# Edges of a graph kernel laid out on 128 partitions by 1568 columns instead of 125 by 1600

## What is computed

```
src[200000], dst[200000]: node numbers;  edge_weight1[200000, 1]: edge length
deg   = segment_sum(1, dst) + 1
agg   = segment_sum(h[src] * norm[:, None], dst)            # twice; message layer alike
alpha = softmax over the edges of a dst; out = segment_sum(h[src] * alpha, dst)
logit = q[src] . k[dst] + silu(len * We1 + be1) @ We2 + be2  # softmax over the edges of a src
out   = segment_sum(v[dst] * softmax(logit) * cut(len), src)
```

## Time and profile before

| what | value |
|---|---|
| median of three runs | 23871.3 us |
| span of the profiled execution | 20599.5 us |
| POOL busy | 13905.9 us, 68% of the span |
| first scatter phase, POOL's first to last DMA | 566.1 to 3111.1 us |
| second scatter phase, POOL's first to last DMA | 3119.1 to 5549.0 us |

### The profile page before, as it was taken

How to read it: one execution, slowest core, us unless ns; L and a number is a source line. 1 busy time by engine, 2 the same in 40 slices (tenths; PEclk the granted TensorE clock), 3 DMA queues, 4 the chain that set the end, 5 groups by cost and what they waited for, 6 DMA issues and landing times. The chain is left out here.

```text
span 20599.5 us, 263453 instructions
## 1 busy us (share of the span) xinstructions
PE 11568.2 (56%) x38052; PEld 7949.2 (39%) x38053; DVE 9032.9 (44%) x32383; ACT 3681.9 (18%) x13726; POOL 13905.9 (68%) x14023
## 2 busy tenths in 40 slices
PE   4452005666644443444377778998477757734444
PEld 1221003333333333333222227888444446633333
DVE  7894000000133333333477776555455556643332
ACT  0000001111100000000088882222111111100000
POOL 0787777777667774777477777777377764437774
PEclk8655555555555555555599995555555556655555
DMA  0000000000112222222210002222355553312222
GB/s 19 1 2 2 2 2 10 2 2 2 13 49 53 53 53 40 53 52 53 30 8 2 2 2 48 54 54 54 76 157 156 157 126 100 100 34 53 53 53 39
DMA packets 955238, 936.26 MB, mean 45 GB/s; under 512 B 316676, under 2 KB 792417, under 8 KB 954328
## 3 DMA queue, kind: packets, MB, share of 16 engines
q0 software_dynamic: 448512, 670.29, 16.4%
q1 hardware_dynamic: 506112, 260.47, 4.7%
q10 hardware_dynamic: 576, 5.11, 0.1%
HBM read 788.96 MB, written 142.48 MB: 45 GB/s over the span
## 5 line engine op out<-in xcount | busy, mean ns | idle before, releaser
L941 PE MATMUL banks<-room 128*128 128x128 f32 (+2 forms) x16640 | 4717.8, 440 | 3647.6 <-DMA room<-tab,stage 3229.5
L847 POOL DMA_INDIRECT room<-tab,stage x4992 | 4710.4, 944 | 2189.1 <-issue 1513.5
L941 PEld LDWEIGHTS banks<-room 128*128 128x128 f32 x16640 | 3802.2, 316 | 4499.0 <-DVE room L954 2419.1
L964 DVE TENSOR_TENSOR acc<-acc,banks 128x128 f32 (+2 forms) x4160 | 1209.2, 291 | 5088.1 <-PE banks L941 4484.8
L954 DVE TENSOR_SCALAR room<-ramp,loc 128x128 f32<-128x128 f32 x11648 | 3173.8, 331 | 80.5 <-issue 66.0
L419 POOL DMA_INDIRECT by_src<-room,stage x1600 | 2058.9, 1287 | 1051.4 <-ACT room L410 567.5
L419 POOL DMA_INDIRECT by_dst<-room,stage x1600 | 1905.0, 1191 | 532.9 <-issue 487.0
L847 POOL DMA_INDIRECT acc<-tab_kv,stage x1664 | 1580.2, 950 | 785.1 <-issue 498.6
L847 POOL DMA_INDIRECT room<-tab_a,stage x1664 | 1571.6, 944 | 755.8 <-issue 405.0
L847 POOL DMA_INDIRECT room<-tab_h,stage x1664 | 1575.1, 947 | 535.5 <-issue 500.8
L939 PE MATMUL banks<-acc,room 128*128 128x512 f32 x3328 | 1627.4, 611 | 497.7 <-ACT acc L887 451.3
(11 more groups left out here) (263 smaller groups left out, 11748.5 us busy)
## 6 DMA issues: line engine op xcount, KB each, us to landing
value_rows<-acc SPq DMA_DIRECT2D x416, 256.0 KB, 3.0
room<-value_rows SPq DMA_DIRECT2D x416, 256.0 KB, 2.9
room<-tab,stage POOLq DMA_INDIRECT x4992
room<-tab_a,stage POOLq DMA_INDIRECT x1664
room<-tab_h,stage POOLq DMA_INDIRECT x1664
acc<-tab_kv,stage POOLq DMA_INDIRECT x1664
by_src<-room,stage POOLq DMA_INDIRECT x1600, 2.6
by_dst<-room,stage POOLq DMA_INDIRECT x1600, 2.6
```

The costliest lines, as they stand in the source:

```text
L847: pool.indirect_dma_start(far[:, m, 0:row], None, table, bass.IndirectOffsetOnAxis(k.stage[:, m:m + 1], axis=0)).then_inc(k.gathered[m], 16)
L941: last = pe.matmul(agg[j % SUM_RING][:, 0:width], oh, k.gat[:, ring(j) + t, 0:width], start=(t == 0), stop=(t == G - 1))
L964: dve.tensor_tensor(mine, mine, agg[j % SUM_RING][:, 0:width], ALU.add).then_inc(added, 1)
```

## The change

EP becomes 128 and EC 1568. 128 * 1568 is 200704, so 704 entries of the last row are padding: their node number is NP = 6272, which is block 49, a fiftieth block (NB1 = 50), and their local number gets PAD added. Both loops of `Rank` take 50 turns; the scatter loops take 98 turns of 16 DMAs with 128 rows each. The lists in DRAM get TD = 1672 rows a partition, of which the readers take the first 1664. The core of the diff:

```
-EP = 125
-EC = E // EP
+EP = P
+EC = 1568
+LAST = E - (EP - 1) * EC
+NB1 = NB + 1
+TD = T + 8
...
-            load(k.raw_s, a["src"].rearrange("(p c) -> p c", p=EP))
-            load(k.raw_d, a["dst"].rearrange("(p c) -> p c", p=EP))
-            load(k.w_f, a["edge_weight1"].rearrange("(p c) o -> p (c o)", p=EP))
+            w = a["edge_weight1"].rearrange("e o -> (e o)")
+            full = (EP - 1) * EC
+
+            def load_rows(dst, src, lo, up):
+                load(dst[lo:up, :], src[lo * EC:up * EC].rearrange("(p c) -> p c", c=EC))
+            for dst, src in ((k.raw_s, a["src"]), (k.raw_d, a["dst"]), (k.w_f, w)):
+                load_rows(dst, src, 0, 96)
+            sp.wait_ge(padded, 3)
+            for dst, src in ((k.raw_s, a["src"]), (k.raw_d, a["dst"]), (k.w_f, w)):
+                load_rows(dst, src, 96, EP - 1)
+                load(dst[EP - 1:EP, 0:LAST], src[full:E].rearrange("(o c) -> o c", o=1))
...
+            dve.memset(k.raw_s[96:EP, :], NP).then_inc(padded, 1)
+            dve.memset(k.raw_d[96:EP, :], NP).then_inc(padded, 1)
+            dve.memset(k.w_f[96:EP, :], 0.0).then_inc(padded, 1)
...
-                dve.tensor_copy(full, raw)
+                link(dve, dve.tensor_scalar(full, raw, float(NP - 1), None, ALU.min))
...
+                link(dve, dve.tensor_scalar(k.mask, hi, float(NB), PAD, ALU.is_ge, ALU.mult))
+                link(dve, dve.tensor_tensor(loc, loc, k.mask, ALU.add))
...
-        with dve.Fori(0, NB) as b:
+        with dve.Fori(0, NB1) as b:
             link.loop(b, 2)
...
-        link(dve, dve.scalar_tensor_tensor(slot, k.posf, float(T), k.scan, ALU.mult, ALU.add))
+        link(dve, dve.scalar_tensor_tensor(slot, k.posf, float(TD), k.scan, ALU.mult, ALU.add))
...
-            sp.dma_start(rec, source.rearrange("(p t) f -> p t f", p=P)).then_inc(loaded, 16)
+            sp.dma_start(rec, source.rearrange("(p t) f -> p t f", p=P)[:, 0:T, :]).then_inc(loaded, 16)
```

More of the change, by code:

```diff
@@ L56 @@
 ROUND = 12582912.0
-assert NB % BC == 0 and EP * EC == E and EC % BODY == 0 and T % P == 0
+assert NB % BC == 0 and 0 < LAST <= EC and EC % (2 * BODY) == 0 and T % P == 0
+assert E + NB * (GE - 1) + EP * EC - E <= P * TD
 MATS = ("L0_gnn_W1", "L0_gnn_Wt1", "L0_gnn_W2", "L0_gnn_Wt2", "L1_gnn_W", "L2_gnn_Wq", "L2_gnn_Wk",
@@ L118, in allocate @@
     k.sem = phase_sem
-    k.by_dst_dram = dram("by_dst", (P * T, 2))
-    k.by_src_dram = dram("by_src", (P * T, 4))
+    k.by_dst_dram = dram("by_dst", (P * TD, 2))
+    k.by_src_dram = dram("by_src", (P * TD, 4))
     k.w_rows_dram = dram("w_rows", (T, P))
@@ L201, in load_phase @@
     a = k.a
-    loaded, iotas, filled, zero_done = (k.sem(n) for n in ("loaded", "iotas", "filled", "zero_done"))
+    loaded, iotas, filled, zero_done, padded = (k.sem(n) for n in ("loaded", "iotas", "filled", "zero_done", "padded"))
     link = Link(k.sem("const_step"))
@@ L235, in _ @@
             act.wait_ge(filled, 2)
-            half = P * T // 2 // P
+            half = TD // 2
             rows = k.by_src_dram.rearrange("(p s r) f -> p s (r f)", p=P, s=2)
@@ L301, in tensor @@
         pe.wait_ge(self.counted, 1)
-        pe.matmul(ps[0][:, 0:NB], k.ones[0:EP, :], cnt[0:EP, :], start=True, stop=True)
-        pe.matmul(ps[1][0:EP, 0:NB], k.below[0:EP, 0:EP], cnt[0:EP, :], start=True, stop=True)
-        pe.matmul(ps[2][0:NB, 0:1], cnt[0:EP, :], k.ones[0:EP, 0:1], start=True, stop=True)\
+        pe.matmul(ps[0][:, 0:NB1], k.ones[0:EP, :], cnt[0:EP, :], start=True, stop=True)
+        pe.matmul(ps[1][0:EP, 0:NB1], k.below[0:EP, 0:EP], cnt[0:EP, :], start=True, stop=True)
+        pe.matmul(ps[2][0:NB, 0:1], cnt[0:EP, 0:NB], k.ones[0:EP, 0:1], start=True, stop=True)\
             .then_inc(self.summed, 1)
@@ L322, in tensor @@
         add(k.zeros, True, False)
-        with pe.Fori(0, NB) as b:
+        with pe.Fori(0, NB1) as b:
             pe.wait_ge(self.picked, b + 1)
@@ L339, in vector @@
                                         ALU.add, accum_out=cnt[0:EP, bass.ds(b, 1)]))
[L340 removed]
+        link.end(NB1)
         dve.sem_inc(self.counted, 1)
         dve.wait_ge(self.summed, 1)
[L344 removed]
+        link(dve, dve.tensor_scalar(tot_i, ps[0][:, 0:NB1], float(GE - 1), None, ALU.add))
         link(dve, dve.tensor_scalar(tot_i, tot_i, GSH, None, ALU.arith_shift_right))
         link(dve, dve.tensor_copy(tot, tot_i))
[L347 removed]
+        link(dve, dve.tensor_tensor_scan(pre[0:EP, :], tot[0:EP, :], k.zeros[:, 0:NB1], 0.0, ALU.add, ALU.add))
         link(dve, dve.tensor_tensor(pre[0:EP, :], pre[0:EP, :], tot[0:EP, :], ALU.subtract))
[L349 removed]
+        link(dve, dve.scalar_tensor_tensor(k.offs[0:EP, :], pre[0:EP, :], float(GE), ps[1][0:EP, 0:NB1],
                                            ALU.mult, ALU.add))
@@ L371, in vector @@
             dve.wait_ge(self.picked, b + 1)
-        link.end(NB)
-        dve.wait_ge(self.merged, NB + 2)
+        link.end(NB1)
+        dve.wait_ge(self.merged, NB1 + 2)
         for m, (lo, up) in enumerate(self.spans):
```

10 lines of the change are left out of this document (5 added, 5 removed).

## The result

Forecast 23099 us; measured 24109.42 us (median of four runs, 24058.15 to 24139.83) beside 23860.01 for the kernel before (four runs, 23844.28 to 23878.32): a ratio of 1.0108, with an interval of 1.0091 to 1.0124. The change made the kernel 1.1% slower, where 3.2% faster had been forecast, and the time lies above the range.

What follows compares the result with a forecast made beforehand. POOL's cost per indirect DMA was taken to bound the scatter phases; -397 - 392 + 10 + 6 + 1 = -772 us, taken from 23871, gave 23099 us (3.2% faster), range 22900 to 23290.

Steps and rivals of the forecast that it cites:

- The rival that scaled the rest: Whole kernel: unprofiled runs are slower throughout by 1.159, so the gain is 895 us and the time 22976; chance 0.15.
- POOL is the bound: Scatter phases: where undisturbed, a phase is mainly the number of DMAs times POOL's cost of one, 1.490 us each.
- 2.4 us of cover per half: Second scatter phase: ACT needs 7.6 us plus 0.5 per half of 8 DMAs, POOL 9.98, so POOL stays the bound.
- Scatter of 128 rows: Both scatter phases: each DMA costs what a gather does, 1.247 us apart instead of 1.490, with 0.942 of work.
- The filler: Scatters of 125 rows: 5 queues carry 25 rows each, 11 get 4-byte fillers, so POOL writes 400 elements against 128.
- First phase: First scatter phase: 1568 DMAs at 1.247 us plus 194 us lost, 2149 us, a change of -397 us.
- Second phase: Second scatter phase: POOL's part changes by -426 us and the bias tail by +34, together -392 us.
- Its opening: Start of the second scatter phase: 16 staged DMAs, then a wait for ACT until 69.9 us after the first; unchanged.
- Its tail: End of the second scatter phase: bias steps run on behind POOL's end, 70.0 us instead of 35.8, so +34.
- Load: Loading the lists at the start: uneven row shares among DMA engines and DVE's memsets add 10 us.
- Start of the scatters: Everything ahead of the first scatter: load +10, fields +6 and Rank "src" +1 us.
- Sum: Whole kernel: all terms together give -772 us, a span of 19827, with the time outside the span unchanged.

Runs made afterwards that it cites:

- e1: The kernel before, unedited, profiled once more: 24371.96 us, beside 24378.31 for the kernel before on that chip.
- e18: The changed kernel, unedited, on another chip, one without slow issue: 19917.63 us, beside 20641.27 for the kernel before.
- e6: The changed kernel with each scatter cut to rows 0 to 119 of its 128: 24611.76 us, beside 24408.88 for the kernel before.
- e15: The kernel before with three short POOL memsets ahead of every gather of the passes: 23387.43 us, beside 23852.46 for the kernel before.
- e17: The changed kernel with three short POOL memsets ahead of every scatter and every gather: 23483.2 us, ratio 0.9645 to the kernel before.
- e3: The changed kernel with each scatter cut to rows 0 to 111 of its 128: 24570.74 us, beside 24378.31 for the kernel before.

## Why the prediction was wrong, step by step

**The step that failed** is the one that carried the sum from the span to the time: "The page gives no time of its own for the profiled execution, and the median stands 3272 us above the span. I take that rest as unchanged". There is no such rest. The kernel before spends its 24372 us inside its span too (e1: 24370.1). The 3272 us are slow issue, which the first trace doesn't have, and nearly all of it lies in the passes: from the first gather on, the first trace has 14857.8 us and e1, with a span 3771 us longer, 18634.2. The rival that scaled the rest failed with it, since it also took this trace as a picture of the timed runs. The rows on which I built "POOL is the bound" were true only of the other kind of chip.

**What was wrong in consequence**, where slow issue is: POOL is the bound of the first scatter phase only as long as the degree loop ends first. With a scatter every 1.49 us the loop has 846 us to spare (2258 against 3104, e1). With one every 1.26 us it ends 550 us behind POOL. That is +289 us where -397 was forecast. In the second phase the forecast had 2.4 us of cover per half, and had named a wait of POOL for ACT inside it as the sign of too thin a cover. POOL waited for ACT's staging some 341 us there (894.5 in all, less the 553.4 of the gap; e1 has 46), so -51 instead of -392. The start gave +14 where +17 was forecast.

**The terms themselves**, against e18, where the condition under which I had worked them out holds:
- Scatter of 128 rows: forecast 0.942 us of work and 1.247 apart; measured 0.962 and 500 / 393 = 1.272. Right in kind (the upper bound was 1.52), low by 0.025 us. 3120 of them are 78 us, more than the miss below; beside `Rank` less was lost than forecast.
- The filler: right in its bytes. In all but e6, work went with 16 times the rows of one queue: 0.942 us for 112 rows (7 per queue), 0.959 for 128 (8), 0.987 for 100 (10), 1.081 for 119 (17), 1.187 for 125 (25). e6 doesn't fit (0.993 for 120, 8 per queue), so this rule of cost isn't the whole of it.
- First phase, from its first DMA to the second phase's first: 2186.1 against 2553.0, -367 (forecast -397). Three DMAs per turn passed beside `Rank`, as forecast.
- Second phase, to the first gather: 5040.0 - 2764.3 = 2275.7 against 2622.6, -347 (forecast -392). Its opening: POOL goes on 69.5 us after its first DMA (forecast 69.9). Its tail: last bias addition at 4884.6, 69.8 us after POOL's last DMA ended at 4814.8 (forecast 70.0).
- Load: fields start at 63.37, +10.1 (forecast +10). Start of the scatters: +12 (forecast +17).
- Sum: up to the first gather -702 (5040.0 against 5741.7), in time -724 beside the kernel before on e18's chip, in span -684 against the first profile (forecast -772). On this kind of chip a forecast of 3.7% stands against 3.3 to 3.5% measured.

So for chips without slow issue the mechanism and its prices were right. The sign of the answer was wrong, because the time to be forecast was that of another regime than the trace, in which the degree loop and not POOL ends the first scatter phase.

**What stays open.** What inside the chip makes the engines issue slowly while POOL's indirect DMAs follow each other closely, and whether their distance is all that counts, isn't shown. The instruction queue has 29 packets both in after and in e18, 28 both in e1 and in the first profile, so no more code is loaded where issue is slow. The parts of such a DMA, POOL's own work, the transfer and its completion, were not tried apart. That distance matters is seen in `Rank` and in the degree loop; for the passes there is only e15 and e17. Nor is it known what makes a chip of one kind or the other.

## What to carry to other kernels

Lay the span of a profile beside the time of that same execution, and beside the median, before anything is built on it. If they differ by per cents, the trace shows another regime, and a difference carried over as a constant is a guess. When one engine of a phase is made faster, ask of every other engine in that phase how much room it has left under the new rate, for the dear form may have been a pause that the others lived on. And a cheaper DMA pays where the issuing engine is the bound in the runs that are timed; here the same edit is worth -3.5% on a chip of one kind, and +0.4 to +1.1% in the three measurements on chips of the other.

## What the runs showed of the hardware that was not expected

- The same program takes 20.6 ms on two chips and 23.9 to 24.4 on three, at nearly equal mean granted clocks (0.577 to 0.578 and 0.572 to 0.576), and on the three the engines issue slowly beside POOL's indirect DMAs. A register instruction of 57 ns then takes up to 2098.
- On those chips slower is faster: three memsets ahead of each gather gave 465 us (e15), ahead of all indirect DMAs 879 us against the kernel before (e17).
- Beside the counting loop of `Rank`, DVE passes 58 instructions in 110 us with scatters 1.25 us apart (e3) and 98 with scatters 1.30 apart (e6), on one chip.
- A POOL DMA of 128 scattered rows costs 0.959 us and a gather of 128 rows of 512 bytes 0.945: direction and bytes hardly matter to POOL here.
